# A fused decoder layer on one core: TensorE's per-pair products behind both projection units of a step instead of between them, and one weight conversion two steps sooner

## The reference, cut to what matters

```python
proj = layernorm(x) @ in_proj_w.T           # gate, xBC and dt
xBC  = silu(conv(xBC) + conv_b)             # depthwise, 4 taps, causal
hs, Bm, Cm = split(xBC)                     # 128 heads of 64; 8 groups, 128 states
dt   = softplus(dt + dt_bias); cum = cumsum(dt * A)
y    = sum_j (C_i . B_j) * exp(cum_i - cum_j) * dt_j * hs_j  + D * hs   # j <= i
g    = y * silu(gate)
g    = g * rsqrt(mean(g*g over a group of 1024) + eps) * norm_w
x    = x + g @ out_w.T
```

## Time and profile before

| what | value |
|---|---|
| median of 3 runs | 2824.62 us (2821.0 to 2827.11) |
| the profiled execution | 2825.73 us, span 2823.9 us |
| mean granted TensorE clock | 0.996 |
| TensorE busy | 2791.2 us, 99% |
| weight loads busy | 2264.8 us, 80% |
| VectorE / ScalarE / GpSimd busy | 2015.0 / 1462.5 / 1313.9 us (71 / 52 / 47%) |
| DMA | 578.39 MB, mean 205 GB/s |

### The profile page before, as it was taken

One profiled execution on the slowest core, in us unless ns is written; L12 is line 12 of the kernel. 1 busy time (PEld: TensorE's weight loads), 2 busy tenths in 40 slices (PEclk: granted clock), 3 DMA queues, 4 the chain that ended last, 5 costly groups with the idle time before them and its releaser, 6 DMA issues.

```text
span 2823.9 us, 56343 instructions
## 1 busy us (share of the span) xinstructions
PE 2791.2 (99%) x22190; PEld 2264.8 (80%) x22190; DVE 2015.0 (71%) x3213; ACT 1462.5 (52%) x2205; POOL 1313.9 (47%) x842
## 2 busy tenths in 40 slices
PE   7999999999999999999999999999999999999998
PEld 5788888778788888887888888888888888878886
DVE  8777768887667667677676776677766666666667
ACT  5566666655454545455354454454544445453545
POOL 4667767775343433443334443434434344443344
PEclk9999999999999999999999999999999999999999
DMA  7788777878565565565655565555655656556530
GB/s 257 265 303 300 266 268 259 283 258 294 176 194 183 184 196 171 195 197 179 206 192 188 191 193 173 189 182 188 203 188 190 195 176 199 183 183 196 183 136 31
DMA packets 179508, 578.39 MB, mean 205 GB/s; under 512 B 25264, under 2 KB 31920, under 8 KB 171184
## 3 DMA queue, kind: packets, MB, share of 16 engines
q1 hardware_dynamic: 179248, 574.79, 61.8%
HBM read 460.42 MB, written 114.29 MB: 204 GB/s over the span
## 4 chain that ended last, share of the span: by engine, by line
PE 91%; DVE 6%; ACT 1%; issue 1%; DMA 0%; POOL 0%; SPq 0%; DVEq 0%; ACTq 0%; POOLq 0%
PE p_in L482 53%; PE p_out L482 24%; PE p_y L482 8%; PE p_in L584 4%; DVE cv L1464 1%; PE p_y L722 1%; DVE o_ring L1404 1%; PE p_y L827 0%; DVE t_y L1513 0%; DVE mx L1653 0%; DVE g_f L1525 0%; ACT L970 0%; DMA raw_w<-wt 0%; DVE cum L1426 0%; DVE sc L1640 0%
## 5 line engine op out<-in xcount | busy, mean ns | idle before, releaser
L482 PE MATMUL p_in<-xnb,w_ring 128*128 128x512 f32 x6864 | 1676.9, 397 | 1.8 <-DVE x_tok L1501 0.9
L482 PEld LDWEIGHTS p_in<-xnb,w_ring 128*128 128x128 f32 x6864 | 1263.5, 189 | 263.3 <-issue 2.2
L1464 DVE SCALAR_TENSOR_TENSOR cv<-p_in,cpar,cv 128x504 f32<-128x504 f32 x954 | 699.9, 734 | 458.5 <-ACT cv L970 434.9
L1915 POOL TENSOR_TENSOR g_lo<-g_f,g_hi 128x512 fp32r<-128x512 f32 x256 | 338.9, 1325 | 1178.3 <-ACT g_hi L970 1178.3
L482 PE MATMUL p_out<-o_ring,g_hi 128*128 128x512 f32 x2048 | 639.2, 393 | 1.7 <-POOL g_lo L1915 1.7
L970 ACT ACTIVATE cv<-p_in,cpar 128x512 f32<-128x512 f32 x318 | 246.7, 776 | 621.8 <-PE p_in L482 585.5
L482 PEld LDWEIGHTS p_out<-o_ring,g_hi 128*128 128x128 f32 x2048 | 379.9, 188 | 80.1 <-issue 2.3
L482 PE MATMUL p_out<-o_ring,g_lo 128*128 128x512 f32 x1024 | 400.1, 391 | 0.0
L1501 DVE TENSOR_TENSOR x_tok<-p_in,dts 128x512 f32<-128x512 f32 x256 | 176.6, 690 | 259.8 <-PE p_in L584 258.4
L970 ACT ACTIVATE x_t<-cv 128x512 f32<-128x512 f32 x256 | 160.8, 628 | 312.3 <-DVE t_y L1513 288.9
L1926 POOL TENSOR_TENSOR ss<-ss,g_sq 128x512 f32<-128x512 f32 x190 | 309.4, 1628 | 7.5
(11 more groups left out here) (273 smaller groups left out, 2253.8 us busy)
## 6 DMA issues: line engine op xcount, KB each, us to landing
w_ring<-ws_scr SPq DMA_DIRECT2D x432, 512.0 KB, 3.7
o_ring<-ows_scr SPq DMA_DIRECT2D x192, 512.0 KB, 4.7
ws_scr<-w_ring SPq DMA_DIRECT2D x144, 512.0 KB, 5.9
decay<-cum_scr SPq DMA_DIRECT2D x126, 512.0 KB, 6.7
raw_w<-wt SPq DMA_DIRECT2D x144, 256.0 KB, 5.2
ows_scr<-o_ring SPq DMA_DIRECT2D x64, 512.0 KB, 6.2
raw_o<-owt SPq DMA_DIRECT2D x64, 256.5 KB, 5.4
xt<-x SPq DMA_DIRECT2D x12, 256.0 KB, 8.3
```

The lines of the kernel that those rows point to most:

```text
L482: return nc.tensor.matmul(o, lhsT=l, rhs=r, start=first, stop=last)
L1464: ins = V.scalar_tensor_tensor(acc[:, :, t:SEQ], src[:, :, 0:SEQ - t], cpar[:, 5 * m + 3 - t:5 * m + 4 - t], acc[:, :, t:SEQ], ALU.mult, A ...
L1915: T(g_lo[:, c % 2, :], g_f[:, c % 2, :], g_hi[:, c % 2, :].bitcast(F32), ALU.subtract).then_inc(glo_done, 1)
```

## The change

In all passes but the first, TensorE's heads in steps 2, 4 and 6 come behind unit G instead of between units X and G. The heads of the pair 6, 7 stay where they are. On VectorE the conversion of the experts' weights goes from step 3 of pass 8 to step 1 of pass 8, behind x_tokens(1) and clamped(1) and ahead of conv(4), with a wait for the last weight split.

```diff
--- before.py
+++ after.py
@@ -865,11 +865,13 @@
                 for k in range(2, CPG):
                     if begun or k > 3:
                         unit(2 + 2 * k, tb, g, n)
-                    if k % 2 == 0:
+                    if k % 2 == 0 and not begun:
                         heads(k - 2, tb, g, n)
                     unit(3 + 2 * k, tb, g, n)
                     if k == 2 and not begun:
                         unit(8, tb, g, n)
+                    if k % 2 == 0 and begun:
+                        heads(k - 2, tb, g, n)
                     if final(n) and k == CPG - 1:
                         project(k - 3, tb, n, range(0, 2))
                     elif k >= 3:
@@ -1562,9 +1564,6 @@
                 t, u, tile = opening(tb, g), closing(tb, g), coming(tb, g)
                 S = loop_tile
                 if k == 3 and t is not None:
-                    if t == 0:
-                        dve.wait_ge(post_const, 16 * 8)
-                        expert_weights(S)
                     dve.wait_ge(acc_done, GROUPS * tb)
                     moments_of(S, acb[:, (tb - 1) % 2, t % QT, :]).then_inc(var1_done, 1)
                 if k == 4 and former(t) is not None:
@@ -1820,6 +1819,10 @@
                         refill_o(k)
                     if k == 1:
                         clamped(1, n)
+                    if k == 1 and opening(tb, g) == 0:
+                        dve.wait_ge(post_const, 16 * 8)
+                        dve.wait_ge(wlo_done, UNITS * GROUPS)
+                        expert_weights(loop_tile)
                     if k == 2 and begun:
                         accumulate(*back)
                     late(k, tb, g)
```

## The result

| what | before | after |
|---|---|---|
| median of 5 runs each (3 of them for the table before, with the same median) | 2824.62 us (2821.0 to 2827.11) | 2846.91 us (2844.84 to 2847.24) |
| the profiled execution, its span | 2825.73, 2823.9 us | 2845.37, 2843.6 us |
| mean granted TensorE clock | 0.996 | 0.998 |

The ratio is 1.0078 with a 95% interval of 1.0067 to 1.0089: the changed kernel is 22.3 us slower, where +23.8 was forecast.

A forecast was written before the change was run, and what follows sets the result against it. TensorE holds 91% of the span, so delays that make it wait cost time. Step 2 +24.8, block 0 +2.8, experts' weights -3.8 sum to +23.8 us: median 2848.4 us, range 2837 to 2862.

The forecast's parts named there:

- Step 2: Moved heads make t_y and to_tokens(2) 0.84 us later in 29 passes, 0.2 in two others: 24.8 us slower.
- steps 4 and 6 cost nothing outside block 0: A whole project (2.72 us) and often a slot cover the chain there; 1.9 us of slack take the 0.84: cost 0.
- block 0: Smaller slack without slots: a wait of 0.4 us in step 7, 2.8 us for seven passes, ends 0 and 5.9.
- the experts' weights: Pass 8: conversion moved into VectorE's idle time removes 2.17 us of TensorE idle and the clock fall: -3.8 us.
- The heads of step 4 are also one unit later, which alone would cover the 2.17: Pass 8: the later heads by themselves would cover TensorE's 2.17 us of idle time ahead of them.
- 0.26 of it was missing already: Before to_tokens(2) in step 2: the 0.26 us idle of weight loads was read as a wait, growing to 1.10.
- the forecast's own range: 2840 to 2857 us; 0.58 us per step 2 takes off 8, block 0 and experts put on 7, runs differ by 3.
- rival 2: Entry to and exit from the heads: array switch cheaper beside project, up to 45.6 us back, 2803 us; chance 4%.
- passes 15 and 23: conv(4) is late by itself there, the wait is already 0.90 us, so only 0.2 us is added in each.
- Rival 1: The clock falls at the new waits, 1.6 us each, 31 passes 50 us, so 2898 us; chance 4%.
- Rival 3: No stall, t_y is not bound by the heads; only the experts' weights' gain is left, 2820.8 us; chance 6%.
- Rival 4: Decay load comes too late in block 0: 2.7 us in seven passes, 19 us more, 2867 us; chance 2%.

The follow-up runs named there:

- run 4: Changed kernel with only the heads of step 2 moved, those of steps 4 and 6 left between X and G: 2845.65 us, ratio 1.0078 to the kernel before.
- run 1: Kernel before with only the conversion of the experts' weights moved, heads left between X and G: 2819.9 us, ratio 0.9988 to the kernel before.
- Run 3: Changed kernel with heads of step 2 left between X and G, experts' weights still moved: 2822.55 us, ratio 0.9997 to the kernel before.
- Run 2: Changed kernel with the experts' conversion back in step 3 of pass 8, so only the heads move: 2847.7 us, ratio 1.0086 to the kernel before.
- run 6: Changed kernel with the heads of step 2 behind the half project too: 2916.51 us, ratio 1.0329 to the kernel before.
- run 8: Kernel before with experts' weights in step 1, three x_t slots and no empty wait in slot(2): 2819.77 us, ratio 0.9985 to the kernel before.

## Why the prediction was right

**Right: the place and the size of the loss.** Step 2 was put at 24.8 us; the distances between matmuls grew by 24.9, and run 4 less run 1 is 25.8. Each link is in the trace: heads at X + 5.63 to 5.67 (5.64 predicted), t_y 1.23 us behind them, 2.23 from there to the transposes, an idle time of 1.11 us (1.10 predicted).

**Right but for two places: steps 4 and 6 cost nothing outside block 0.** The weight loads of the transposes of step 4 of pass 16 have no idle time in the kernel after, though t_y waits 0.75 us there as well. The two places are the heads between passes 14 and 15 and between passes 22 and 23. The prediction says that outside pass 8 no wait ahead of heads is over 0.35 us; at these two it was 0.51 already. In the kernel after it is 0.91 and 1.09, and by matmul starts they cost 0.44 and 0.61 us. Run 3, which moves only the heads of steps 4 and 6, has the same two (0.43 and 0.62 over run 1).

**Right in kind, too large: block 0.** The idle time of the weight loads before to_tokens(7) of passes 1 to 7 went from 1.3 to 3.5 us, where 2.8 us of loss stood. By matmul starts it is less: +1.3 us, and +1.1 in run 3 over run 1. Pass 3 was read well (0.4 forecast, 0.36 measured), but it was no pass like the others. Passes 4 and 6 lost 0.75 and 0.84, passes 1, 2 and 7 nothing, and in pass 5 a wait of the kernel before was 0.61 shorter (as in run 1, where no heads had moved). Pass 3, the weight loads:

```profile
352.64 0.42 PEld L584 LDWEIGHTS p_in<-id_sb,x_t 128*128 128x128 f32 x4 [0.62 <-ACT x_t L972]
```

**Right: the experts' weights.** -3.8 was predicted. Run 1 has -3.9 by medians, with an interval of -5.9 to -0.8. By itself it shortens pass 8 by 3.2 us, as 0.51 us of the wait is left. Pass 8 of the changed kernel, less the 0.85 us of its step 2, is 3.7 us shorter.

**Wrong in a side claim: "The heads of step 4 are also one unit later, which alone would cover the 2.17".** Run 2 has 1.45 us of it before unit G. By pass 8 of run 2 the later heads bring 2.1 us in all (88.5 and the 0.85 of step 2, less 87.2), where the claim had 3.8. By run 6's price of a fall, some 1.5 of these are the clock, which did not fall there.

**Wrong in reading: "0.26 of it was missing already".** It was a lead of the weight load, and the chain was just long enough to reach the transposes (0.02 us late, run 8). The increment of 0.84 came from two t_y times and not from this row, so the sum did not feel it. The lower end of the forecast's own range did: "if the 0.26 were no wait", it had the step at 0.58. It is no wait, and the step still costs 0.85. The 0.35 us ahead of the heads is such a lead in part too: X takes 2.92 us to the heads where twelve matmuls take 2.72, so 0.20 us are lost there, and the most that rival 2 could have won was 0.34 us a time and not 0.49.

**Right: passes 15 and 23, "only 0.2 us is added".** It is 0.20 in step 2 of each (0.90 to 1.10 from matmul to matmul), and next to nothing in their other steps.

**The sum.** Within the passes it stood at 23.8 and came to 23.6: 24.9 for step 2, 1.05 for the two places, 1.3 for block 0 and -3.7 for pass 8, 23.6 together. That it is so near is luck in part, as block 0 was put 1.5 us too high and the two places at nothing.

**The rivals.** Rival 1 (the clock falls at the new waits) did not happen here and happened in run 6. Rival 2 (a cheaper switch) is out: 0.35 us of idle weight loads stand ahead of the heads, 1.09 us lie between their start and project, and the first two matmuls of project take 0.57 us where two take 0.45. Rival 3 (no stall) is out by run 4. Rival 4 (the decay load late in block 0) left no trace: passes 1 to 7 grew by 7.4 us, of which 5.9 are step 2 and 1.3 the waits before to_tokens(7). One comparison of the prediction was uneven: the 2.17 us of pass 8 are idle matmuls, the 1.16 and the 1.10 idle weight loads, which in pass 8 idled for 2.56.

**What stays open.** Why the clock falls behind 18 of 31 equal idle times in run 6 and not behind the others. And whether step 3 would bind without its table load and exp: no run took these away.

## What to carry to other kernels

Cost a moved producer from the start of its consumer's series, not from the producer's own work: TensorE did the same matmuls in the same time, and each pass still lost the 0.84 us by which t_y slipped, because only half a project lay over the rest of the series. When such a wait is taken away, look at the next use of the same series before you count the gain; here a third slot took away 26.9 us of waiting in step 2 and gained 6.6 us. And for lost time compare the starts of matmuls, since idle time of weight loads can be nothing but their lead.

## What the runs showed of the hardware

- In passes 1 to 31 the clock fell behind idle times of the matmuls of 2.17 us (one, in the kernel before) and 2.29 us (18 of 31, in run 6). It did not fall behind the one of 1.45 us in run 2, nor behind any of the 31 of 0.70 us in the kernel after. A fall is 3.41 us at 0.50 and costs about 1.5 us.
- The same gap does not always bring it: 13 of 31 times in run 6 it had no effect.
- VectorE's start behind the heads was 1.23 us in step 2 of all 31 passes, whatever TensorE did next: project behind them, or nothing.
